# Attention and mixture of experts on one core: value products of two steps as one block of eight matmuls

## What is computed

```
x = x + xattn(layernorm(x), ctx, mask)       # softmax over 512 source positions, 16 heads
x = x + ffn(layernorm(x))                    # 8 experts, the best 2 of each row, 512 -> 2*352 -> 512
q = Wq t + bq;  k = Wk s + bk;  v = Wv s + bv
dot = (q.k) / 4, masked;  amap = softmax(dot) * mask;  out = amap v
```

## Time and profile before

| | |
|---|---|
| median of 3 runs | 868.2 us (867.61 to 870.95) |
| the profiled execution | 871.53 us, span 869.7 us |
| mean granted clock of TensorE | 0.972 |
| TensorE busy | 801.8 us, 92% of the span |
| VectorE busy | 553.6 us, 64% |
| ScalarE busy | 318.6 us, 37% |
| POOL busy | 370.3 us, 43% |

### The profile page before, as it was taken

One profiled execution on the slowest core, in us unless ns is written; L12 is line 12 of the kernel. 1 busy time (PEld: TensorE's weight loads), 2 busy tenths in 40 slices (PEclk: granted clock), 3 DMA queues, 4 the chain that ended last, 5 costly groups with the idle time before them and its releaser, 6 DMA issues. The chain is left out here.

```text
span 869.7 us, 13002 instructions
## 1 busy us (share of the span) xinstructions
PE 801.8 (92%) x3757; PEld 365.1 (42%) x3758; DVE 553.6 (64%) x1071; ACT 318.6 (37%) x619; POOL 370.3 (43%) x392
## 2 busy tenths in 40 slices
PE   5888898989999998999989988899999999999993
PEld 2322332333333433433333332365555665665661
DVE  5778887889888887888877874445433333333331
ACT  0035465556565565665655666522000000000000
POOL 7544364556565655655745423334211221211221
PEclk9579999999999999999999999999999999999997
DMA  6745577666766866856845542354648546354332
GB/s 188 231 129 145 172 203 221 200 209 210 231 206 184 264 196 182 257 163 177 244 127 160 172 113 83 94 144 110 152 89 227 133 110 172 65 156 72 72 51 34
DMA packets 84524, 138.02 MB, mean 159 GB/s; under 512 B 14765, under 2 KB 40685, under 8 KB 84474
## 3 DMA queue, kind: packets, MB, share of 16 engines
q1 hardware_dynamic: 68970, 108.65, 41.8%
q0 software_dynamic: 7744, 17.86, 10.7%
q10 hardware_dynamic: 7760, 10.89, 4.5%
HBM read 77.36 MB, written 59.36 MB: 157 GB/s over the span
## 5 line engine op out<-in xcount | busy, mean ns | idle before, releaser
L843 ACT ACTIVATE pr<-sc 128x512 f32<-128x512 f32 x512 | 267.1, 603 | 219.5 <-PE sc L1507 219.3
L990 DVE TENSOR_REDUCE mx<-tile 128x2 f32<-128x1024 f32 x256 | 309.0, 1216 | 55.9 <-PE tile L1519 50.3
L1507 PE MATMUL sc<-qk 100*128 100x512 bf16 x512 | 154.8, 384 | 9.9 <-DMA qk<-mxt 7.2
L1519 PE MATMUL tile<-qk 97*128 97x512 bf16 x496 | 150.9, 388 | 14.0 <-DVE mx L990 7.9
L765 POOL DMA_INDIRECT out_dram<-xin,ids x36 | 56.4, 1566 | 224.0 <-DVE ids L1312 220.0
L1545 PE MATMUL pvb<-pr,vp 128*32 128x512 f32 x1024 | 138.0, 611 | 0.0
L1660 PE MATMUL pvb<-wring,qkf 128*128 (+1 forms) x216 | 98.7, 593 | 1.6 <-DVE qkf L1322 1.6
L720 POOL TENSOR_SCALAR parts<-qkf 128x512 bf16<-128x512 f32 x31 | 46.9, 1512 | 123.3 <-DVE qkf L1074 119.3
L1519 PEld LDWEIGHTS tile<-qk 97*128 97x128 bf16 x496 | 35.0, 98 | 145.6 <-issue 75.7
L1639 PE MATMUL tile<-wring,xh 128*128 x288 | 91.3, 460 | 0.0
L1639 PE MATMUL sc<-wring,xh 128*128 x288 | 91.2, 459 | 0.0
(11 more groups left out here) (158 smaller groups left out, 789.1 us busy)
## 6 DMA issues: line engine op xcount, KB each, us to landing
qk<-stack_d SPq DMA_DIRECT2D x32, 768.0 KB
stack_d<-parts SPq DMA_DIRECT2D x32, 384.0 KB, 3.1
wring<-w_dram SPq DMA_DIRECT2D x32, 352.0 KB, 7.2
cin<-routed_d ACTq DMA_DIRECT2D x36, 257.0 KB, 3.6
stack_d<-parts SPq DMA_DIRECT2D x32, 256.0 KB, 3.1
pv_d<-ov SPq DMA_DIRECT2D x32, 256.0 KB, 3.4
xin<-x_dram SPq DMA_DIRECT2D x16, 256.0 KB, 5.4
cin<-ctxt_dram SPq DMA_DIRECT2D x8, 512.0 KB, 6.3
```

The lines of the kernel that those rows point to most:

```text
L843: nc.scalar.activation(pr[s % 2][:, j, :], sc[(32 * u + 4 * s + j) % NSC][:, :], ACT.Exp, scale=SCALE).then_inc(exped.sem, 1)
L990: dve.tensor_reduce(cols, t[:, :, :], X, ALU.max, negate=True).then_inc(drained.sem, 1)
L1507: nc.tensor.matmul(sc[(32 * u + 4 * s + j) % NSC][:, :], ks[half(u)][0:ALL_ROWS, h, c * P:c * P + P], qs[half(u)][0:ALL_ROWS, h, :], start ...
L1519: last = nc.tensor.matmul(t[:, i, :], qs[half(w)][0:RAW_ROWS, h, c * P:c * P + P], ks[half(w)][0:RAW_ROWS, h, :], start=True, stop=True)
```

## The change

The product of a step is no longer issued in every step. In steps 2, 4 and 6 the products s - 2 and s - 1 follow each other, and products 6 and 7 stand in step 0 of the next unit (for the last unit, behind the first gate matmuls). So eight matmuls stand in one block in every second step. `pr` gets a third buffer. The values of the next unit move from step 0 to step 1 (they stood there already in unit 0), the logits from step 4 to step 5. VectorE's order follows: values out behind the token statistics, batch statistics one pair of maxima earlier, the choice of experts behind the maxima of step 5. To make room in SBUF for the third buffer, the two mask buffers now lie in `ov`.

```diff
--- before.py
+++ after.py
@@ -46,7 +46,8 @@
 CHUNKS = 6
 NPAIR = 16
 LEAD = 4
-VALUES_AT = 1, 0
+VALUES_AT = 1
+NPR = 3
 NSLOT = 2
 TAIL = UNITS - 1
 EARLY_PLANNED, PADS_PLANNED, ROWS_PLANNED, ALL_PLANNED = 22, 24, 39, 49
@@ -121,8 +122,8 @@
 
 def fillers(n, s):
 
-    return ((["v"] if s == VALUES_AT[n > 0] and has(n + 1) else []) + (["q"] if s == 3 and has(n + 3) else [])
-            + (["xT"] if s == 3 and has(n - 2) else []) + (["logits"] if s == 4 and has(n - 2) else []))
+    return ((["v"] if s == VALUES_AT and has(n + 1) else []) + (["q"] if s == 3 and has(n + 3) else [])
+            + (["xT"] if s == 3 and has(n - 2) else []) + (["logits"] if s == 5 and has(n - 2) else []))
 
 
 def tile_events(n):
@@ -234,8 +235,6 @@
         bqk = sb("bqk", [P, 2, 2])
         bv_s = sb("bv_s", [P, C])
         gate_s = sb("gate_s", [P, 4, E])
-        mall = sb("mall", [B, T])
-        mrow = sb("mrow", [B, 2, T], BF16)
         mc = sb("mc", [P, B, 4])
         md = sb("md", [P, B, 32])
         xin = sb("xin", [P, 2, T])
@@ -249,8 +248,10 @@
         qk = [sb(f"qk{i}", [P, 2, UH, T], BF16) for i in range(2)]
         qs, ks = ([t[:, side] for t in qk] for side in range(2))
         vp = [sb(f"vp{i}", [P, 4, UH, 32]) for i in range(2)]
-        pr = [sb(f"pr{i}", [P, 4, T]) for i in range(2)]
+        pr = [sb(f"pr{i}", [P, 4, T]) for i in range(NPR)]
         ov = sb("ov", [P, 2, T])
+        mall = ov[0:B, 0, :]
+        mrow = ov[0:B, 1, :].bitcast(BF16).rearrange("b (s t) -> b s t", s=2)
         mx = sb("mx", [P, 2, 32])
         mxr = sb("mxr", [32, P])
         mxt = sb("mxt", [32, 3, P], BF16)
@@ -381,7 +382,7 @@
                  (bqk[:, 0, :], bq, wq_in),
                  (wk_s[:, :, :], wk.rearrange("(c p) o -> p c o", p=P), wk_in),
                  (bqk[:, 1, :], bk, wk_in),
-                 (mall[:, :], mask, mask_in))
+                 (mall, mask, mask_in))
         const = ((idf[:, :], ident),
                  (wv_s[:, :, :], wv.rearrange("(c p) o -> p c o", p=P)),
                  (bv_s[:, :], bv.rearrange("(o c) -> o c", o=1).broadcast_to([P, C])),
@@ -838,9 +839,9 @@
                         if has(u):
                             act.wait_ge(scored.sem, scored.at(u, (s, j)))
 
-                            if j == 0 and (due := pved.at(u, s, back=2)) is not None:
+                            if j == 0 and (due := pved.at(u, s, back=NPR)) is not None:
                                 act.wait_ge(pved.sem, due)
-                            nc.scalar.activation(pr[s % 2][:, j, :], sc[(32 * u + 4 * s + j) % NSC][:, :],
+                            nc.scalar.activation(pr[(8 * u + s) % NPR][:, j, :], sc[(32 * u + 4 * s + j) % NSC][:, :],
                                                  ACT.Exp, scale=SCALE).then_inc(exped.sem, 1)
                         if (s, j) == (4, 0) and has(u - 2):
                             transposed_out(u)
@@ -1124,10 +1125,10 @@
                 for m in (0, 1, 2):
                     maximum(1, 2, m)
                 normalize(0)
-                values_out(1)
 
                 for m in (3, 4, 5):
                     maximum(1, 2, m)
+                values_out(1)
                 split_maxima(1, 1, 1)
 
                 for m in (6, 7, 8, 9):
@@ -1158,12 +1159,12 @@
                 maximum(u, u + 1, 4)
                 normalize(u - 1)
                 maximum(u, u + 1, 5)
-                values_out(u)
 
                 maximum(u, u + 1, 6)
                 token_stats(u, 0)
                 maximum(u, u + 1, 7)
                 token_stats(u, 1)
+                values_out(u)
 
                 maximum(u, u + 1, 8)
                 token_normalize(u, 0)
@@ -1179,22 +1180,23 @@
                 projection_out(u, 0)
 
                 maximum(u, u + 1, 12)
+                batch_stats(u, 0)
                 maximum(u, u + 1, 13)
-                choose(u, 0)
-                choose(u, 1)
-                choose(u, 2)
-                choose(u, 3)
+                batch_stats(u, 1)
 
                 maximum(u, u + 1, 14)
-                batch_stats(u, 0)
                 maximum(u, u + 1, 15)
-                batch_stats(u, 1)
-                choose(u, 4)
-                choose(u, 5)
+                for step in range(4):
+                    choose(u, step)
                 if u == TAIL:
+                    choose(u, 4)
+                    choose(u, 5)
                     fetch(0, 0)
 
                 maximum(u, u + 2, 0)
+                if u < TAIL:
+                    choose(u, 4)
+                    choose(u, 5)
                 maximum(u, u + 2, 1)
                 split_maxima(u, u + 1, ALL)
 
@@ -1543,7 +1545,7 @@
                 pe.wait_ge(exped.sem, exped.at(u, (s, 3)))
                 for i in range(4):
                     last = nc.tensor.matmul(pvb[32 * i:32 * i + 32, :], vp[half(u)][:, c, 4 * g + i, :],
-                                            pr[s % 2][:, i, :], start=(c == 0), stop=(c == 3))
+                                            pr[(8 * u + s) % NPR][:, i, :], start=(c == 0), stop=(c == 3))
                 last.then_inc(pved.sem, 1)
 
             def project(u, side):
@@ -1674,14 +1676,16 @@
                     if has(u):
                         scores(u, s, 3)
                     if s == 0 and has(u - 1):
+                        product(u - 1, 6)
                         product(u - 1, 7)
-                    if s and has(u):
+                    if s in (2, 4, 6) and has(u):
+                        product(u, s - 2)
                         product(u, s - 1)
                     if s == 7:
                         ranks(u)
                     for w, m in todo[1:]:
                         raw_scores(u, w, m)
-                    if s == VALUES_AT[u > 0]:
+                    if s == VALUES_AT:
                         values(u)
                     if u == 0 and s == 0:
                         project(-1, 1)
@@ -1692,7 +1696,7 @@
                         transpose_tokens(u)
                     if u == TAIL and s == 2:
                         count_early()
-                    if s == 4:
+                    if s == 5:
                         logits(u)
                     if u == TAIL and s == 5:
                         transpose_rows(0, 0)
@@ -1743,6 +1747,7 @@
             for e in range(WRING):
                 pe.wait_ge(weights_in[e], 16 * CHUNKS)
             off = gate(0, 0)
+            product(TAIL, 6)
             product(TAIL, 7)
             transpose_rows(1, 1)
             expand(0, off, up[0], I, up_done)
```

## The result

The changed kernel takes 922.16 us, median of 4 runs (920.46 to 925.69), against 869.58 beside it: a ratio of 1.062 (95%: 1.058 to 1.065), 52.6 us more. The profiled execution took 920.51 us, its span is 918.7, and the mean granted clock of TensorE 0.963, where it was 0.972.

The account below looks back on a forecast made before the run. TensorE was taken to set the pace, VectorE having only a sixth of its time free. 868.2 + 35.7 (27 + 2 + 2.2 + 3.0 + 1.5) = 904 us, range 880 to 918.

Parts of the forecast that it names:

- The block's saving: Joined block of eight products takes 1.91 us instead of 2 x 1.00; saves 0.18 a pair of steps, bounds 0 and 0.24.
- the rival in which they don't: The two halves of a block still drain between: no saving, +11.5 on the forecast, 915 us; chance 0.08.
- The slots: Two shared PSUM slots drained late by VectorE: pairs of steps lose 0.70, 0.93, 0.70 and 0.94, unit 34.2 instead of 30.92.
- The least wait of 0.88: Filler after the odd step's raw pairs: VectorE needs 3.07 us where TensorE leaves 2.19, so each waits at least 0.88.
- smaller loss: VectorE uses its idle time at the blocks better; each pair loses only 0.70: +20, 888 us; chance 0.17.
- faster: Unit bound by TensorE's own work, slots free in time: some 853 to 857 us; chance 0.07.
- The six late transposes: Maxima transposes in six units wait about 1 us behind late reductions, batch statistics and choice of experts; mostly vanish: -6.
- Ten units: +27: Steady units 3 to 12: +3.3 each gives +33, less 6 for late transposes that vanish.
- rival of late transfers: The maxima's transfer, just hidden in the walk, is late in all ten units: 10 x 1 more, 914 us; chance 0.1.
- Units 13 and 14: +2.2 and +3.0: Unit 13, without query and key, takes 32.35 against 30.18; unit 14 takes 31.45 against 28.47.
- Unit 15: 0: No raw pairs; ScalarE's exponentials set a pair of steps to 5.2 to 5.5, but transposes and logits fall into that: 0.
- Before unit 3: +3.5: Unit 0 loses 0, unit 1 +1.5, unit 2 +2, where a stall on its stack transfer absorbs part.

Follow-up runs that it names:

- The cheaper reduction: Each maximum taken over the first 256 of 512 columns, in both kernels: the changed kernel 868.52 us (0.999), the kernel before 848.58 us (0.977).
- the waits filled: Changed kernel plus unused constant matmuls in TensorE's waits of units 2 to 14 and at the ends of units 13 and 14: 911.66 us, ratio 1.049.

## Why the prediction was wrong

The sign and the mechanism held, the size didn't: 922 instead of 904, outside the range.

- **The block's saving.** Expected: 1.91 us from a block to what follows it, and 0.18 saved a pair of steps (4 x 0.45 + 0.10 is 1.90, which changes nothing). Measured: 1.86 (the row's 1.92 runs on to the end of the last record), and 2 x 1.00 + 0.09 - 1.86 = 0.23 a pair; 0.24 in the pairs without a filler. That is close to the upper bound that I gave: four rounds take less than 4 x 0.45. The halves join, so the rival in which they don't is out.
- **The slots.** Expected 0.70, 0.93, 0.70 and 0.94 a pair, the unit 34.2. Measured 8.20, 9.01, 7.35 and 9.52 against my 8.16, 9.08, 7.21 and 9.74, the unit 34.08. The cheaper reduction gives 33 us of the loss back. The least wait of 0.88 shows in its two parts: the odd step's second pair follows the first by 0.84 instead of 0.66, and the values that pair by 1.12 instead of 0.44, 0.86 together. The rival "smaller loss" is out: no pair lost less than 9.52 - 8.80 = 0.72. So is "faster", whose low end should have been 851 (868.2 - 11.5 - 6), not 853.
- **The six late transposes.** Expected -6, and their waits are gone. Their cause was another than the one I named: ahead of each of the six, a small operation of VectorE that started beside a product of POOL had lasted 1.1 to 1.3 us (last section).
- **Ten units: +27.** Measured +30.8. The steady unit loses 3.17, so ten lose 31.7 and not 33. Above ten steady units the kernel before has 8.7 us (late transposes and two late transfers), the changed one 7.8: two steps at half clock, 1.65 each in units 4 and 12, and units 3, 6 and 11 longer by 1.2 to 1.6 with their late transfers. That is 31.7 - 8.7 + 7.8. The rival of late transfers, in all ten units, is out: the scores wait for them 3.8 us in all, where they waited 3.2.
- **Units 13 and 14: +2.2 and +3.0.** Measured +3.7 and +4.0, with half clock in both (5.44 instead of 3.80 for step 6 of unit 13, 5.33 instead of 3.69 for step 0 of unit 14).
- **Unit 15: 0.** This is the single term that failed most: +5.6. I let TensorE's own work stay 4.8 us a pair and let ScalarE set 5.2 to 5.5. In the trace steps 0 and 2 take 5.3 each, where they take 3.25 and 3.68 at full clock, with the waits filled. The wait of 2.83 ahead of them is followed by half clock. The kernel before waited 2.69 there and was slowed too, but less: its granted clock in the unit is 0.93, here 0.80. With the waits filled it is 0.93 again and the unit loses 2.0, so 3.6 of the 5.6 are the clock. The other 2.0 remain without it, and I had them at nothing.
- **Before unit 3: +3.5**, measured +3.7.
- **No term for the granted clock.** This is the step of the working that failed. I read 1.00 in the steady stretch before and took it as given. With waits of 0.5 to 1.1 us in every odd step it falls now and then, and a block there costs 1.6 us more. Of the 49.0 us between the traces the sum has 35.7 and misses 13.3; 10.1 of these are the clock (3.3 in units 4 and 12, 1.6 in unit 13, 1.6 in unit 14, 3.6 in unit 15). The filled waits give back 11 to 13 us. With them the ten units lose 26.8 us (344.63 against 317.82), where I had 27. What is left, 911.7, is 7.7 above my sum; in that trace the excess lies before unit 3 (+5.7, I had +3.5), in unit 15 (+2.0) and behind it (+1.8).

The runs show that the block costs some 45 us in this order. The drain's length accounts for 33 us of the loss and the clock for 11 to 13, and the two overlap: where the wait goes, the low clock goes as well. It is not settled why the clock falls behind one wait and not behind the next of equal length, nor which units lose their blocks in a given execution. Ahead of unit 14 the kernel before waited 1.40 (504.85) and stayed at full clock; the changed one waited 1.37 and did not. A third slot, the direct cure for the waits, wasn't tried: a slot takes two PSUM banks, and slots, scores and products already use eight.

The Trainium skill, TensorEngine Tiling (Array Packing), Key Properties, says that a change of tiling mode drains TensorE. The trace agrees, with 0.23 us saved a pair, and by that rule alone the kernel would be 64 x 0.23 = 15 us faster; no run here shows the whole kernel gain by it.

## What to carry to other kernels

Before work is bunched on one engine, compare the time that its buffers need to be drained with the gaps that are left: spacing is what lets a two-slot pipeline with a 1.2 us drain keep up, and a saving of 0.2 us isn't worth a wait of 0.7. A new wait can have a second price, the granted clock behind it: walk the waits, then ask what runs behind each at half clock. And judge a drain's place by trying it in the kernel without the change too, since a better order may cost when the work is spread.

## What else the runs showed

Filling a wait with useless matmuls pays here: 911.7 us against 922.2 and 926.7, with the same unit of 34.08. Among executions of the changed kernel the time goes with the mean granted clock: 920.5 us at 0.963, 925.7 at 0.956, 934.3 at 0.948.

Some small operations of VectorE that start while a `tensor_tensor` of POOL runs end just after it. The changed kernel, both engines at once:

```profile
327.15 1.28 POOL L736 TENSOR_TENSOR att<-num,rb 128x512 f32<-128x512 f32 x1 [1.99 <-DMA rb<-recip_d]
327.17 1.29 DVE L1030 CAST i8f<-i 128x8 f32<-128x8 uint32 x1
```

The kernel before, where it made the maxima's transpose late:

```profile
401.74 1.28 POOL L735 TENSOR_TENSOR att<-num,rb 128x512 f32<-128x512 f32 x1 [1.61 <-DMA rb<-recip_d]
...
401.87 1.19 DVE L1032 TENSOR_TENSOR sel<-io,i8f 128x16 f32<-128x16 f32 x1
...
404.53 0.27 PE L1626 MATMUL tile<-idf,mx 128*32 128x128 f32 x1 [1.10 <-DVE mx L990]
```

Such operations on 8 or 16 columns take 0.17 us elsewhere. Not every operation is held: in the kernel before, the aggregate at 401.78 takes its 0.17 beside the same product, and the reduction from PSUM isn't longer than others (1.21 to 1.23). The ones held in the traces are casts and `tensor_tensor`s between tiles in SBUF, and they end 0.02 to 0.15 us after POOL's product. In the run with fillers in the even steps and single products this makes the split some 1.1 us longer in most units (1.38 for L1020 at 311.56). I found this only after the prediction, and didn't test it by itself.
